# Loading keys and values in pieces, and splitting the row transfers between two queues, in a two-layer attention and expert kernel

## Time and profile before

| | |
|---|---|
| median of 3 runs | 2059.43 us (2053.86 to 2059.93) |
| the profiled execution | 2055.51 us; its span 2053.7 us |
| mean granted clock of TensorE | 0.923 of full |
| busy in the span | PE 1757.6 us (86%), DVE 1329.9 (65%), ACT 1195.0 (58%), POOL 1142.0 (56%) |
| stages, from the span's start | token stage 0 to 211 us, attention 0 to about 1165 (its last unit to 1188), token stage 1 to 1496, attention 1 to the end |

### The profile page before, as it was taken

The page is one execution under the profiler, slowest core; times in us unless marked ns, Lnnn a source line. Parts: engine busy times, 40 slices in busy tenths (PEclk is TensorE's granted clock), DMA queues, the critical chain, the costliest instruction groups (busy, mean ns, idle before and its releaser), DMA issues. The chain is left out here.

```text
span 2053.7 us, 78601 instructions
## 1 busy us (share of the span) xinstructions
PE 1757.6 (86%) x34080; PEld 1323.3 (64%) x34080; DVE 1329.9 (65%) x1965; ACT 1195.0 (58%) x1438; POOL 1142.0 (56%) x1502
## 2 busy tenths in 40 slices
PE   6876699898898979989998769999969879789886
PEld 4665577777787767777877546666735545455554
DVE  5543577767677657877777334454477868777883
ACT  2322387777677757877877623444426646566555
POOL 4743479986799859997898621212012334334343
PEclk8888799999999989999999879999969989989998
DMA  3456312223221241222211121233220121211100
GB/s 99 125 155 190 107 54 60 68 68 97 71 69 49 67 121 46 63 66 64 68 45 52 61 90 53 83 86 86 69 57 23 30 63 31 48 44 28 30 23 16
DMA packets 166300, 139.90 MB, mean 68 GB/s; under 512 B 91715, under 2 KB 157014, under 8 KB 160454
## 3 DMA queue, kind: packets, MB, share of 16 engines
q1 hardware_dynamic: 153370, 105.87, 18.0%
q10 hardware_dynamic: 7212, 16.42, 3.3%
q0 software_dynamic: 5376, 12.59, 2.2%
HBM read 90.91 MB, written 43.12 MB: 65 GB/s over the span
## 5 line engine op out<-in xcount | busy, mean ns | idle before, releaser
L1348 ACT ACTIVATE a_EX<-bank 128x1024 f32<-128x1024 f32 x624 | 615.0, 1026 | 286.6 <-PE bank L1217 219.6
L1469 DVE TENSOR_TENSOR a_PM<-bank,a_PM 128x1024 f32<-128x1024 f32 x336 | 401.7, 1222 | 169.1 <-PE bank L1217 157.3
L1297 POOL TENSOR_TENSOR a_SN<-a_SN,a_MB 128x1024 f32<-128x1024 f32 x176 | 421.0, 2430 | 46.3 <-DMA a_MB<-m_dram 45.2
L1492 DVE TENSOR_REDUCE a_M<-bank 128x2 f32<-128x1024 f32 (+3 forms) x304 | 342.1, 1165 | 73.1 <-PE bank L1230 47.7
L1432 PE MATMUL bank<-a_EX,VV 128*32 128x128 f32 x9984 | 358.2, 287 | 4.5 <-issue 3.0
L1217 PE MATMUL bank<-QS,KS 51*128 51x128 bf16 (+1 forms) x4992 | 238.1, 229 | 98.1 <-DMA QS<-a_MP 48.0
L1432 PEld LDWEIGHTS bank<-a_EX,VV 128*32 128x32 f32 x9984 | 269.0, 114 | 57.2 <-issue 28.3
L1217 PEld LDWEIGHTS bank<-QS,KS 51*128 51x128 bf16 (+1 forms) x4992 | 159.2, 100 | 193.2 <-issue 59.8
L1344 ACT ACTIVATE a_SN<-bank 128x1024 f32<-128x1024 f32 x176 | 177.0, 1026 | 75.2 <-PE bank L1196 74.3
L1352 ACT ACTIVATE a_SN<-a_SN 128x1024 f32<-128x1024 f32 x176 | 185.2, 1058 | 36.6 <-POOL a_SN L1297 36.2
L1196 PE MATMUL bank<-QP,rel_t 112*128 112x32 bf16 x5632 | 198.5, 177 | 7.3 <-issue 7.0
(11 more groups left out here) (159 smaller groups left out, 2460.3 us busy)
## 6 DMA issues: line engine op xcount, KB each, us to landing
a_MB<-m_dram SPq DMA_DIRECT2D x32, 1024.0 KB, 5.0
QS<-q_dram SPq DMA_DIRECT2D x192, 96.0 KB, 3.0
KS<-k_dram ACTq DMA_DIRECT2D x12, 768.0 KB
q_dram<-t_PARTS SPq DMA_DIRECT2D x32, 192.0 KB, 2.8
k_dram<-t_PARTS SPq DMA_DIRECT2D x16, 384.0 KB, 2.9
QS<-a_MP SPq DMA_DIRECT2D x384, 2.0 KB
q_dram<-t_PARTS SPq DMA_DIRECT2D x32, 128.0 KB, 2.6
k_dram<-t_PARTS SPq DMA_DIRECT2D x16, 256.0 KB, 2.9
```

The source lines that it names most:

```text
L1297: pool.tensor_tensor(near_view(sn), near_view(sn), as_near(MB[:, :, :], it.part), ALU.add)\
L1348: act.activation(as_banks(EX[:, it.need % ER[layer]], part), by_head, ACT.Exp, scale=SCALE).then_inc(act_done, 1)
L1469: dve.tensor_tensor(pm, mb.rearrange("p hh (k i) -> p hh k i", k=4), pm, ALU.max).then_inc(max_used, 1)
L1492: dve.tensor_reduce(target.rearrange("p (hh k) -> p hh k", hh=2)[:, :, p0:p0 + g], mb[:, :, 0:g * width].rearrange("p hh (k j) -> p hh k j ...
```

## The change

1. **Pieces.** `load_kv` is gone. SyncE loads batch b + 1 in pieces behind the reloads of the first four units of batch b (three in layer 1): half of KS, the other half, the values, both halves of KR. Where the buffer was used by the batch before, SyncE first waits for that batch's last product with the values. ScalarE issues nothing, at the start of the stage neither. The Exp of the lambda sums moves from there to ScalarE's first ocopy.
2. **Rows.** In layer 1 SyncE issues three of the six row transfers of a unit and GpSimd, once its own split is done, the other three, on semaphores of their own (m_in2) that the exp scores also wait for.
3. **x.** X has two buffers; groups 0 and 1 are fetched at once, later ones as before but a group further ahead. For layer 1 both are fetched near the end of attention 0.
4. **Token order.** Layer 0 stores x in natural order; layer 1 works in it and stores its output as it is. The mask's output is now adjacent columns.
5. **Plan.** New costs for the moved steps and other aims.

```diff
+def feeds(layer, u):
+    return u % NB < 4 - layer and u // NB + 1 < B
...
-    {"max": (-0.89, 0.93), "mrow": (-5, -1.11), "msplit": (-2.16, -1.22), "exp": (1.31, 0.71),
-     "av": (4.53, -0.91), "out": (2.07, 1.41)}]
-NEAR_BY, STAY = (179, 493), (0.55, 0.47)
...
+    {"max": (-0.91, 0.98), "mrow": (-3.76, -0.86), "msplit": (-2.02, -2.6), "exp": (1.41, 0.71),
+     "av": (4.47, -0.2), "out": (2.39, 1.09)}]
+NEAR_BY, STAY = (236, 237), (0.59, 0.86)
...
         def load_x(eng, layer, x_src, X, f):
-            eng.dma_start(X[:, :, :], x_src.rearrange("(g t p) d -> g p t d", t=GT, p=P)[f]).then_inc(x_ins[layer], 16)
+            eng.dma_start(X[:, f % 2, :, :], x_src.rearrange("(g t p) d -> g p t d", t=GT, p=P)[f]).then_inc(x_ins[layer][f % 2], 16)
...
+        def load_k(layer, eng, b, hh, far):
+            to, src = (KR, kr_dram) if far else (KS, k_dram)
+            eng.dma_start(to[hh * HALF:hh * HALF + ROWS, b % 2, :, :].rearrange("r p t -> r (p t)"),
+                          src[b][:, hh].rearrange("s d p t -> s d (p t)")).then_inc(kv_in[layer][b % 2], 16)
...
+        def load_piece(layer, eng, b, k):
+            if k < 2:
+                load_k(layer, eng, b, k, False)
+            if k == 2:
+                load_v(layer, eng, b)
+            if k == 3:
                 for hh in range(2):
+                    load_k(layer, eng, b, hh, True)
...
                     def fetch_x(f):
-                        pool.wait_ge(x_free, f)
+                        pool.wait_ge(x_free, f - 1)
...
-                        out_h = bank[:, 2 * it.n + hh, :].rearrange("p (h c a) -> p h c a", h=4, a=2)[:, :, :, half]
+                        out_h = bank[:, 2 * it.n + hh, :].rearrange("p (h a c) -> p h a c", h=4, a=2)[:, :, half, :]
...
+            def store_rows(eng, u, hh, done):
+                for k in range(3):
+                    row = hh * HALF + ROWS + k
+                    eng.dma_start(QS[row:row + 1, u % QR, :, hh, :], MP[hh * PAIRS:(hh + 1) * PAIRS, u % 2, k, :])\
+                       .then_inc(done[u % QR], 16)
...
                         if it.kind == "msplit":
                             sp.wait_ge(m_split, u + 1)
...
+                            store_rows(sp, u, 0, m_in)
+                            if layer == 0:
+                                store_rows(sp, u, 1, m_in)
...
                             sp.wait_ge(act_psum, it.need + 1)
                             load_q(layer, sp, u + QR)
+                            if feeds(layer, u):
+                                if u >= NB:
+                                    sp.wait_ge(av_done, it.room)
+                                load_piece(layer, sp, u // NB + 1, u % NB)
...
                             pool.tensor_tensor(mp[:, 2], MS[:, :], mp[:, 1], ALU.subtract).then_inc(m_split, 1)
+                            if layer == 1:
+                                pool.wait_ge(m_split, u + 1)
+                                store_rows(pool, u, 1, m_in2)
...
                 def _(act):
-                    load_kv(layer, act, 1)
...
-                            if u % NB == NB - 1 and u // NB + 2 < B:
-                                load_kv(layer, act, u // NB + 2)
...
                         elif kind == "exp":
-                            pe.wait_ge(m_in[r], 96 * (u // QR + 1))
+                            pe.wait_ge(m_in[r], (96 - 48 * layer) * (u // QR + 1))
+                            if layer == 1:
+                                pe.wait_ge(m_in2[r], 48 * (u // QR + 1))
```

89 lines of the change are left out of this document (43 added, 46 removed).

## The result

The changed kernel takes 2136.68 us (median of 4 runs, 2132.87 to 2142.89), the one before, beside it, 2057.36 (2053.86 to 2059.93). The ratio is 1.0382, 95% interval 1.0345 to 1.0419: 79 us slower. The forecast was 2012 us, and even rival D, the slower one, said only 2073.

A forecast was written before the change was run, and what follows sets the result against it. Bound by TensorE and GpSimd in layer 0, TensorE and VectorE in layer 1, plus key/value bursts at batch edges. Terms -25.4 - 1.8 + 17 - 11.3 + 1 - 3 - 2 - 4.8 - 13 = -43.3 from 2055.5: 2012 us, range 1981 to 2043.

The forecast's parts named there:

- rival D: Layer 0: pieces on SyncE hold the maxima's store, GpSimd starves, TensorE's clock falls to 0.85; 2073 us, chance 0.06.
- GpSimd's next drain may be held ... Nothing is charged.: Layer 1, GpSimd issuing rows: mean-square step and final addition behind the drain are far from urgent; charged nothing.
- The rows' gain, -3 us: Layer 1: half the rows issued by GpSimd, so both halves land 2 us earlier; -3 us, bounds 0 and 7.3.
- The pieces: SyncE's queue behind reloads: pieces delay the maxima's store and MB; +17 us in layer 0, +1 in layer 1.
- in one lump the same bytes cost 12 to 13 us per batch, not more: Argument against rival D: the bytes of keys and values, loaded as one burst, cost no more than this per batch.
- The bursts go: Batch edges without ScalarE's bursts of keys and values: -25.4 us in layer 0, -11.3 us in layer 1.
- x in two buffers, -4.8 us: Layer 1's token stage: x of group 1 is loaded before the stage, so the keys' matmul no longer waits 4.84 us.
- the start of layer 1, -2: Unit 0 of layer 1: the 9.21 us split stall goes without a burst; -2 us, bounds 0 and -6.
- The mask, -13: Layer 1's causal mask matmuls: adjacent columns save 26 us of TensorE work, half off the time; bounds 0 and -40.
- Half of that: Share of the mask's 26 us of TensorE work taken off the time, TensorE not being alone on layer 1's path.
- The order, 0 (-10 to +10): Planner's moved aims: layer 0's inner units can't gain, no row prices it elsewhere; value 0, bounds -10 and +10.

The follow-up runs named there:

- rows kernel: The kernel before with GpSimd issuing three of the six row transfers in layer 1, planned order unchanged: 2098.44 us, ratio 1.0190.
- plan alone: The kernel before with only the changed kernel's planned order (aims, NEAR_BY, STAY, step costs): 2074.49 us, ratio 1.0088.
- pieces kernel: The kernel before with SyncE loading keys and values in pieces behind its reloads, ScalarE issuing none, planned order unchanged: 2108.72 us, ratio 1.0233.

## Why GpSimd's transfers cost time

Late rows or held drains? Two kernels add three small transfers per unit that nobody reads (rows of a constant to a scratch tensor in DRAM, so nothing of the result depends on them), all six rows staying on SyncE. In one GpSimd issues them, in the other SyncE.

```diff
+                                for k in range(3):
+                                    pool.dma_start(side_dram[3 * u + k], eye[8 * k:8 * k + 8, :]).then_inc(side_out, 16)
...
+                            for k in range(3):
+                                sp.dma_start(side_dram[3 * u + k], eye[8 * k:8 * k + 8, :]).then_inc(side_out, 16)
```

> The kernel before, SyncE issuing all six rows as before; in addition GpSimd waits for its own split in layer 1 and issues three transfers of 4 KB each to a scratch tensor that nobody reads (an addition: it computes nothing). Theory R1 (GpSimd's next drain is held until its own transfers have landed, so the mean-square step behind it is late and TensorE stands in front of the turn of the output): the loss of the rows kernel returns though no row depends on GpSimd, +25 to +45 us (2085 to 2100). Theory R2 (the rows that GpSimd issues land later than SyncE's, and the exp scores wait for them): this kernel costs only issue time, -3 to +8 us.

> The kernel before with the same three dummy transfers per unit of layer 1 as in the kernel with dummies (+42 us), but issued by SyncE behind its six rows. If the loss is GpSimd's held drains, it is gone: 2055 to 2068 us (some issue time behind the rows may show). If the DMA engines' work or the writes to the scratch tensor cost it, it stays: 2090 to 2105.

Measured: on GpSimd 2102.94 us, 1.0210 (1.0180 to 1.0240), +43 us; on SyncE 2057.24 us, 0.9985 (0.9959 to 1.0011), nothing. The same bytes cost nothing unless GpSimd issues them. Waits of layer 1, dummies on GpSimd:

```profile
PE bank L1454 <- POOL a_OF L1323: 44.5, 16, 7.7
POOL a_RS L467 <- issue: 41.2, 32, 5.4
POOL a_MS L1308 <- issue: 38.3, 15, 9.9
```

and on SyncE:

```profile
POOL a_MS L1311 <- issue: 11.7, 9, 2.1
PE bank L1453 <- POOL a_OF L1322: 11.3, 5, 7.7
POOL a_RS L467 <- issue: 10.2, 32, 1.4
```

So GpSimd's drain waits for the transfers that GpSimd has issued, not for its arithmetic alone: away from the start of the stage it holds the second kernel 2.1 us at most, the first 9.9 in the split and 5.4 in the mean-square step beside a burst, and up to 3.2 elsewhere. The landings in the traces show it directly. The fifteen kernels here in which GpSimd loads x and g, before and after included, have 237 idle times of GpSimd of 1.5 us or more put down to "issue", and each of them ends 0.19 to 0.36 us after the last transfer that GpSimd had issued has landed.

The reverse: **GpSimd issues nothing in the attention stages but the load of x for the next stage.** Its two loads per unit (x and g) go to SyncE, behind the final store.

```diff
-                            if u + 2 < UNITS:
-                                load_xg(u + 2)
...
+                            if u + 2 < UNITS:
+                                load_xg(sp, u + 2)
```

> The kernel before with GpSimd's own loads (x and g of a unit, two per unit) issued by SyncE behind the final store; GpSimd then issues no transfer in an attention stage. The opposite of the added transfers that cost 42 us. If a drain of GpSimd waits for GpSimd's own transfers, its idle times put down to issue (in layer 1 11.6 us before the split, 10.4 before the inverse root, 17.0 before the load) and some 1.1 us of issue per unit go, and part of the bursts' harm in layer 1: 2058 less 10 to 30 us. If the drains only wait for its arithmetic and the loss came from the wait on the split or the issue time, no change: 2052 to 2060 us.

Measured: 2034.78 us, 0.9885 (0.9846 to 0.9923), 24 us faster than before by the ratio, as the first theory has it. Its waits in layer 1, of which the split's is gone from the list:

```profile
PE bank L1217 <- DMA QS<-a_MP: 20.8, 3, 10.2
...
PE bank L1443 <- POOL a_OF L1314: 11.0, 4, 8.1
POOL a_RS L465 <- issue: 4.8, 31, 0.2
```

Each attention stage is 6 us shorter in the profiled execution. TensorE's wait for a_OF is what it was (11.0 us against 10.9), its wait for rows fell from 28.3 to 20.8. How much of the gain is the drains and how much the 1.1 us of issue per unit was not separated.

**Is the plan's loss of the same kind?** In the trace of the plan alone the split of a batch's first unit comes right behind GpSimd's loads:

```profile
1786.20 0.58 POOL L1291 DMA_DIRECT2D a_XG<-x_mid  x1 [0.57 <-issue]
1786.79 0.54 POOL L1292 DMA_DIRECT2D a_XG<-g_dram  x1
1788.61 0.28 POOL L1309 CAST a_MP<-a_MR 16x128 bf16<-16x128 f32 x1 [1.28 <-ACTq L1377]
1796.92 0.41 POOL L1311 TENSOR_TENSOR a_MS<-a_MR,a_MP 16x128 f32<-16x128 f32 x1 [8.03 <-issue]
```

The two diffs, of the plan and of the moved loads, together:

> The kernel before with the planned order of the changed kernel (alone +17 us) and GpSimd's own loads on SyncE (alone -21 us). If the order costs because it puts the split of a batch's first unit right behind GpSimd's own loads, whose landing then holds its drain (8.03 us in the trace of the plan alone), the loss goes with them: 2025 to 2038 us, no slower than the moved loads alone. If the order costs in another way, the two add: 2058 + 17 - 21 = 2054 us.

Measured: 2066.25 us, 1.0035 (1.0005 to 1.0065), 31 us more than with the loads moved and the old plan. My guess falls: the drain is gone and the loss is not. Order of time on ScalarE, SyncE and TensorE at the same edge:

```profile
1642.65 1.50 ACTq L554 DMA_DIRECT2D KS<-k_dram  x2
...
1647.11 12.13 SPq L1261 DMA_DIRECT2D QS<-a_MP  x12
...
1665.08 1.04 PE L1224 MATMUL bank<-QS,KS 51*128 51x128 bf16 x16 [13.76 <-DMA QS<-a_MP]
```

The new order puts the rows of two units, twelve issues, into one row behind the burst, where the old one has six, and TensorE waits 13.76 us instead of 9.47. In all TensorE waits 28.0 us for rows in this layer 1, against 20.8 with the loads moved alone: some 7 of the 31 us. Where the rest of the plan's loss comes from was not tried and stays open.

## Why the pieces cost time

In the changed kernel, SyncE at an inner unit behind a key piece and behind the values:

```profile
549.61 0.79 SPq L553 DMA_DIRECT2D KS<-k_dram  x1
550.50 0.65 SPq L1279 DMA_DIRECT2D m_dram<-a_MR  x1
551.58 4.02 SPq L1249 DMA_DIRECT2D QS<-a_MP  x6
561.86 0.33 SPq L1284 DMA_DIRECT2D a_MB<-m_dram  x1
...
583.71 0.61 SPq L557 DMA_DIRECT2D VV<-v_dram  x1
584.45 0.65 SPq L1279 DMA_DIRECT2D m_dram<-a_MR  x1
585.85 4.42 SPq L1249 DMA_DIRECT2D QS<-a_MP  x6
590.39 0.37 SPq L1284 DMA_DIRECT2D a_MB<-m_dram  x1
```

MB waits for the store of the maxima (and for the last addition of the unit before), so the time from the one issue to the other is a bound on that small store: 11.4 us behind keys, 5.9 behind values. The DMA packets in the trace give the store itself (16 packets of 512 bytes): the last of them ends 10.6 us after its issue behind the keys, 3.0 behind the values, and 1.5 to 1.7 where no load of keys or values is beside it. Over layer 0, for the units behind the two key pieces and behind the last piece (in its three batches) that step is (the 9.7 and 9.8 of the kernel before stand behind its bursts, where the store ends after 9.3 and 9.5 us):

| kernel | behind keys 1 | behind keys 2 | behind the last piece | the batches of layer 0, us |
|---|---|---|---|---|
| before (no piece) | 6.1, 9.7, 9.8 | 6.7, 4.8, 8.8 | 8.8, 7.4, 7.4 | 241.6, 241.5, 228.7, 184.9 |
| pieces on SyncE | 10.9, 10.5, 10.7 | 11.9, 11.4, 11.4 | 14.3, 13.1, 14.6 | 251.6, 248.6, 246.9, 186.8 |
| pieces on ScalarE | 10.8, 10.8, 9.7 | 11.0, 12.1, 12.9 | 14.6, 13.1, 14.9 | 256.4, 248.3, 244.8, 182.9 |
| pieces, new key layout | 6.8, 7.6, 7.2 | 7.2, 7.5, 7.6 | 9.1, 8.4, 9.2 | 241.4, 241.9, 231.9, 186.9 |
| the same, issued behind MB | 6.1, 5.3, 4.8 | 5.4, 4.8, 4.9 | 8.8, 8.0, 4.8 | 244.8, 242.6, 237.4, 182.6 |

**Pieces on ScalarE**, behind the last exp of the unit:

```diff
-                                load_piece(layer, sp, u // NB + 1, u % NB)
+                            load_piece(layer, act, it.u // NB + 1, it.u % NB)
```

> The pieces kernel (before + pieces, +48 us) with the same pieces issued by ScalarE instead of SyncE, behind the last exp of the same unit (in three places, where the product that frees the buffer comes later, behind the next output copy); everything else as there. Theory Q (a piece stands ahead of the store of the maxima, the rows and the broadcast on SyncE's own queue, and they can't pass it): on another queue the small transfers pass, and the loss goes: 2050 to 2070 us. Theory E (six DMA engines are full for the 7 us of a key piece, whoever issues it, and the small transfers share these engines): the loss stays, 2090 to 2110 us.

Measured: 2115.66 us, 1.0287 (1.0236 to 1.0338), the loss stays: theory E. What I had written of the queue is wrong in its mechanism: SyncE's small store behind a key piece is as late when ScalarE issues the piece (the store's last packet ends 9.3 to 12.0 us after the store's issue) as when SyncE does (9.9 to 11.1). The kernel before had shown it already, with SyncE's store behind ScalarE's bursts. The rest of the loss has moved in part: GpSimd waits 90.6 us for reloaded queries where it waited 5.0, and 36.0 for MB where it waited 76.7. By the Trainium skill, page "DMA: Bandwidth & Descriptors", section "Queues, rings and completion order", each DMA engine takes turns between the queues that have work for it and drains a whole packet of one queue before it goes to the next, a packet being typically 9 to 17 descriptors and 64 at most. A key piece is 48 rows of 16 KB, by an estimate eight for each of six engines, so by that rule an engine's share can be one packet, which the store can't pass. The trace agrees in so far as the store's first packet, from either queue, starts between 1.6 us before and 1.0 us after the end of the piece's last; it does not show where such packets begin and end. With the section "Rules for kernel authors" of the same page of the Trainium skill, by which spreading over issuing engines saves issue time only, the run agrees.

**A layout for sixteen engines.** The keys' six slots were the outer dimension of a load; now half and slot are swapped in DRAM, so that 48 rows are.

```diff
-        k_dram = dram("k_dram", (B, SLOTS, 2, DH, PAIRS, S), BF16)
+        k_dram = dram("k_dram", (B, 2, SLOTS, DH, PAIRS, S), BF16)
...
-                          src[b][:, hh].rearrange("s d p t -> s d (p t)")).then_inc(kv_in[layer][b % 2], 16)
+                          src[b][hh].rearrange("s d p t -> (s d) (p t)")).then_inc(kv_in[layer][b % 2], 16)
```

> The pieces kernel with k_dram and kr_dram laid out half first, slot second, so that a load's outer dimension on both sides is 48 rows and not 6 slots (the stores of keys become twice as many transfers of half the size). If a load runs on as many engines as divide its outer dimensions, a key piece goes from 6 to 16 engines, from 7.4 us to about 2.8 us, and of the +48 us of the pieces some 18 stay under theory Q and theory E alike: about 2075 us. If the 104 GB/s of a key load has another cause (the memory, the destination), nothing changes: 2105 us.

Measured: 2059.33 us, 0.9984 (0.9961 to 1.0007). The 48 us are gone, where 30 were forecast to go. Windows of the old layout (two times 6 us behind a key piece issued at 556.65) and of the new one (8 us behind one issued at 541.79):

```profile
558.00:564.00 6.00, 6.00 (x209) 5.61 (x209) 3.29 (x4) 4.55 (x5) 4.70 (x4) 1.00 0.47 117
564.00:570.00 6.00, 1.52 (x36) 0.85 (x27) 3.16 (x3) 0.20 (x1) 1.12 (x2) 0.80 0.25 55
```

```profile
542.00:550.00 8.00, 7.75 (x258) 7.02 (x254) 4.79 (x4) 5.87 (x7) 4.68 (x6) 1.00 0.91 145
```

All engines work now (share 0.91 instead of 0.47), but the rate is 145 GB/s, not 16/6 of 104, and the page of the profile gives a key piece 8.6 us from issue to landing (median). For the old layout it gives no landing, so the two are compared by the packets of the trace: the last of a key piece's 48 packets of 16 KB ends 10.8 to 12.1 us after the issue in the old layout and 6.8 to 7.9 in the new one. The piece is faster, by a third and not by 16/6. The busy share agrees with more engines at work, as the Trainium skill's rule on the page named above has it (section "Why a DMA increments its semaphore by 16 and not by 1"); the forecast that the time scales with their number, 2.8 us, does not hold. In the old layout TensorE has 1.52 us of work in the second 6 us and stands for rows. The store of the maxima is still late beside the faster piece, but less: it ends 6.0 to 6.8 us after its issue, where it took 9.9 to 11.1, and the step to MB takes 4.8 to 9.5 us in the kernel before where no load is beside it, so most of the delay disappears in it. TensorE's wait for rows, over both layers, falls from 92.2 us to 42.5 (61.4 in the kernel before). How much of this is the shorter piece and how much the other changes of the layout was not separated.

**The same layout with the bursts of before.**

> The kernel before, with its bursts, and the same new layout of k_dram and kr_dram. If sixteen engines carry the burst, the unit behind it in layer 0 shortens from 41.8 and 43.2 us towards the 29.8 of the one without (by half or more), and the two units in layer 1 from 43 towards 37.5: 2058 less 15 to 35 us. If the small transfers behind a burst are late for its issue and its bytes and not for its six engines, no change: 2058 us, plus the doubled stores.

Measured: 2066.23 us, 1.0022 (1.0000 to 1.0043). No gain; the edges of layer 0 stay at 41.8 and 44.0 us. A burst costs 12 to 15 us there with six engines or sixteen (the edge without one takes 29.8 and 29.3).

**Pieces behind MB**, new layout.

```diff
+                        if it.kind == "mb" and u and feeds(layer, u - 1):
+                            load_piece(layer, sp, (u - 1) // NB + 1, (u - 1) % NB)
```

> The kernel with pieces and the new layout of keys (2059 us, where behind a batch's first units of layer 0 34 and 39 us remain), with the pieces of layer 0 issued behind the broadcast load of the maxima of the next unit (MB) and not behind the reload. If what is left of the pieces' cost is small transfers that start together with a piece, the piece has 20 us to land here before the next ones, and the unit from 7 to 8 falls from 38.7 and 40.8 to 30 to 33 us: 2035 to 2045 us in all. If it is the bytes as such, no change, 2060 us.

Measured: 2054.79 us, 1.0001 (0.9975 to 1.0028). The edge fell as forecast, to 33.2 and 33.0 us, and the store of the maxima is on time (its packets end after 1.5 to 2.0 us), but behind the pieces three units of each batch take 31 to 37 us instead, and the batches come out as long. The second expectation, the bytes as such, fits the total. Against the 228.7 us of the batch that loads nothing before, batches that load keys and values take 9 to 16 us more here and 3 to 13 with the pieces of the new layout behind the reload; what in these units the load holds up was not looked into.

**Do the pieces hurt through GpSimd's drain too?** In the trace of the pieces kernel a permutation is held 4.91 us behind GpSimd's loads, and TensorE stands for its rows soon after:

```profile
561.90 2.07 POOL L530 COPY QP<-QS 48x1024 bf16<-48x1024 bf16 x1
568.88 1.04 POOL L529 COPY QN<-QS 48x1024 bf16<-48x1024 bf16 x1 [4.91 <-issue]
...
570.19 0.61 PE L1232 MATMUL bank<-QS,KS 51*128 51x128 bf16 x8 [4.64 <-DMA QS<-a_MP]
```

The diffs of the pieces and of the moved loads together:

> The kernel before with the pieces on SyncE (old layout, six engines) and GpSimd's own loads moved to SyncE. Alone the pieces cost 48 us and the moved loads bring 21. If the pieces hurt mainly by holding GpSimd's drains behind a key piece (4.9 us before the second copy of a permutation, in the trace of the pieces kernel), most of the 48 goes: 2040 to 2060 us. If they hurt by late rows and maxima, the two add: 2058 + 48 - 21 = 2085, or more, as two more loads stand on SyncE's queue.

Measured: 2089.88 us, 1.0133 (1.0111 to 1.0155): the pieces cost 55 us on top of the moved loads (51 by the ratios), as the second expectation has it. GpSimd's held drains are gone, and its wait for MB has grown from 77 to 134 us in their place (without pieces the moved loads alone raise it from 45 to 74). TensorE's wait for rows is 93.4 us. The pieces hurt by late maxima and late rows; the drain was in their shadow.

## A version that beats both

Two kernels put together the diffs of x and token order and of the moved loads. The first has the pieces in the new layout, behind MB, as well; the second keeps the bursts.

> All that the runs speak for together: x in two buffers and natural token order (-7 us alone), pieces in the new layout behind MB (forecast -15 to -25), GpSimd's loads on SyncE (-10 to -30), all six rows on SyncE, planned order of the kernel before. If they add up: 2005 to 2030 us, under both kernels. If GpSimd's loads on SyncE's queue stand in front of reloads and rows: 2040 to 2060.

> The kernel before with x in two buffers, natural token order and GpSimd's own loads on SyncE; bursts as before, no pieces. If the parts add: 2057 - 7 - 21 = 2029 us, the same as the kernel with all parts (2028), so that pieces in the new layout bring nothing at all. If pieces carry a part of that kernel's gain: 2035 to 2045.

Measured: with pieces in the new layout 2028.07 us, 0.9850 (0.9806 to 0.9895); without pieces 2032.31 us, 0.9853 (0.9816 to 0.9890). Both are 1.5% faster than the kernel before and 5% faster than the changed one, and by these runs the pieces bring nothing that their intervals of 0.4% could show. What carries it is x in two buffers and GpSimd's loads on SyncE, which gave 0.3% and 1.15% alone.

## Why the prediction was wrong, step by step

- **"GpSimd's next drain may be held ... Nothing is charged."** This step failed: it cost 39 us alone, 46 inside the changed kernel and 43 with dummies, where it stood at nothing. With the pieces (next but one) it makes up most of the miss. The stall of 9.21 us was read the earlier trace rows, and that a drain behind own loads is held was guessed rightly. What I got wrong is who waits: the mean-square step was called far from urgent because GpSimd idles 361 us. But the turn of its result stands in TensorE's list ahead of exp scores, and TensorE does nothing else until it comes. An engine's mean idle time says nothing of whether one of its steps is waited for. The wait for a_OF was in the trace of before, too (10.9 us in five times, longest 7.7), and not looked up.
- **The rows' gain, -3 us.** It did not come: TensorE's wait for rows is 30.4 us against 28.3.
- **"The pieces", +17 us (bounds 0 and 40) in layer 0 and +1 (0 and 6) in layer 1.** This step failed by more: with the bursts' gain the pieces stood at -18.7 us and measured +48. By stage they cost +37 and +21 us (in the profiled execution, 6 us above its median); with the bursts' 25.4 and 11.3 added back, that is 62 and 32 us, both outside the bounds. A key piece was taken to be done 8.2 us behind the reload; its last packet ends 10.8 to 12.1 us after the piece's issue. MB was the right place to look and its delays were near the forecast (on average 2 and 5 us behind the two key pieces where 3.0 stood for each, 6 behind the last where 7.5 stood; of the 2, two of the three units compared stood behind a burst before). Left out were the six rows, for which TensorE stands 92.2 us in the pieces kernel, over both layers, against 61.4 before; that layer 1's first units of a batch need their rows at once (TensorE stands 6.5, 10.0 and 10.3 us for rows behind the first key pieces of its three batches); and that a piece at the edge costs a burst's time: in the pieces kernel those edges are 41.4 and 40.6 us, one key piece in place of the whole burst. The argument against rival D, "in one lump the same bytes cost 12 to 13 us per batch, not more", was wrong for this layout: cut into four, they meet the small transfers four times (in the new layout the pieces cost no more than the bursts).
- **"The bursts go", -25.4 and -11.3.** Never shown as a gain of its own: no kernel here loads the bytes without paying for them.
- **x in two buffers, -4.8 us, and the start of layer 1, -2.** The stretch is 8.2 us shorter with this part alone, 9.8 in the changed kernel; over all kernels here it takes 343.4 to 347.8 us with one buffer and 336.5 to 339.7 with two. VectorE's wait of 11.70 us for x and TensorE's of 4.84 are gone from the trace of this part alone. Right for x, and larger than its term. The stall at the start of layer 1 is gone with the pieces alone (0.50 us) but back in the changed kernel (7.37 us), where GpSimd's drain there stands behind its own rows; what the start gained was not measured by itself.
- **The mask, -13.** The mechanism was right (417 to 280 ns), the share on the path was not: nothing of it reached the time. "Half of that" had no row behind it.
- **The order, 0 (-10 to +10).** +18 us alone, outside the bounds; 11 inside the changed kernel. Its cause is open but for some 7 us of waits for rows.
- **Rival D** had the sign and, in layer 0, the late maxima, though not the late rows. The clock did fall, but not to its 0.85: in the stretches with pieces, 278.9 to 437.0, 496.5 to 680.8 and 742.1 to 926.8 us of the changed kernel, it was 0.90, 0.94 and 0.91. It charged layer 1 with 6 us, where the change lost 63.

## What to carry to other kernels

Before an engine is given a transfer, read what it does next and who stands behind that; on GpSimd a drain waits for its own transfers, so a queue that is "idle half the time" is no place for them. Ask of each late step whether an in-order engine has its consumer ahead of useful work, and look for that wait in the trace before pricing it at nothing. A large load cut in pieces is not cheaper by itself: it meets the small urgent transfers more often, on SyncE's queue as on ScalarE's.

## What the runs showed of the hardware

- A GpSimd drain behind GpSimd's own transfers holds the engine until these have landed (237 of 237 idle times of 1.5 us or more ended 0.19 to 0.36 us after the last landing). In layer 1: 2.2 us at most behind two loads in the kernel before away from the start of the stage, 5.4 behind three small stores beside a burst, 7 to 10 behind loads beside a key load. With no transfers of its own the same drains cost 0.2 us.
- The packets of a key load of 768 KB end 10.8 to 12.1 us after its issue in the old layout and 6.8 to 7.9 in the new one (busy share of the DMA engines 0.47 and 0.91 in windows behind the issue). The store of the maxima (8 KB) takes 1.5 to 1.7 us with no load beside it, 9.9 to 11.1 behind the first kind of piece, 6.0 to 6.8 behind the second.
- A small store on SyncE's queue is held by a key load on ScalarE's queue (9.3 to 12.0 us) as long as by one on its own (9.9 to 11.1).
- Matmuls of 256 columns into every second fp32 column of PSUM take 417 ns, into runs of 64 adjacent ones 280.
